# Feed-forward upward product: from one 32-bit product to three 16-bit products over a split activation

## The reference

```python
x = x + _L0_xattn_ref(_layernorm(x), ctx, ctx, Wq, Wk, Wv, Wo)
x = x + _L0_ffn_ref(_layernorm(x), W1, b1, W2, b2)
x = x + _L1_xattn_ref(_layernorm(x), ctx, ctx, mask, ...)
x = x + _L1_ffn_ref(_layernorm(x), ...)          # 8 experts, one per token

def _L0_ffn_ref(x, W1, b1, W2, b2):
    def _quantize(W):
        gamma = jnp.mean(jnp.abs(W))
        return jnp.clip(jnp.round(W / (gamma + EPS)), -1.0, 1.0)
    Wq1, Wq2 = _quantize(W1), _quantize(W2)
    h = relu(einsum('bsd,fd->bsf', x, Wq1) + b1)
    return einsum('bsf,df->bsd', h, Wq2) + b2
```

## Time and profile before

| what | us |
|---|---|
| median of 3 runs | 536.88 (535.7 to 539.16) |
| the profiled execution, its own time | 535.18 |
| its span, first to last instruction | 533.0 |
| PE busy in the span | 459.7 |
| POOL busy in the span | 359.5 |
| mean granted TensorE clock, as a share of full | 0.958 |

### The profile page before, as it was taken

How to read it: one execution, slowest core, us unless ns; L and a number is a source line. 1 busy time by engine, 2 the same in 40 slices (tenths; PEclk the granted TensorE clock), 3 DMA queues, 4 the chain that set the end, 5 groups by cost and what they waited for, 6 DMA issues and landing times.

```text
span 533.0 us, 19424 instructions
## 1 busy us (share of the span) xinstructions
PE 459.7 (86%) x6192; PEld 357.6 (67%) x6192; DVE 380.5 (71%) x1125; ACT 350.0 (66%) x872; POOL 359.5 (67%) x739
## 2 busy tenths in 40 slices
PE   3678999999988799998999999999978615999992
PEld 2456777777766699885566666666655405999991
DVE  6788888888986566535578888898898562555551
ACT  4366788888865556563677788788767713666661
POOL 5788887888842366577667776999986770555552
PEclk9799999999999999999799999999999955999997
DMA  7565445454432930034344444555442233444430
GB/s 182 146 160 147 109 121 124 115 138 114 124 77 59 337 85 0 1 91 104 94 114 119 127 122 113 149 146 146 126 126 70 74 121 86 106 108 108 106 99 23
DMA packets 103996, 60.18 MB, mean 113 GB/s; under 512 B 21234, under 2 KB 100098, under 8 KB 103922
## 3 DMA queue, kind: packets, MB, share of 16 engines
q1 hardware_dynamic: 100562, 51.92, 38.8%
q0 software_dynamic: 2784, 6.82, 3.7%
q10 hardware_dynamic: 576, 0.53, 0.3%
HBM read 20.03 MB, written 8.81 MB: 54 GB/s over the span
## 4 chain that ended last, share of the span: by engine, by line
PE 63%; POOL 11%; issue 8%; DVE 8%; DMA 5%; ACT 2%; SPq 1%; POOLq 0%; DVEq 0%; ACTq 0%
PE bank L702 8%; PE bank L923 6%; PE bank L845 5%; PE score L653 5%; PE scoreT L835 5%; PE scoreT L913 5%; PE bank L561 3%; POOL expert_rows L1341 3%; DVE negmax L1536 3%; PE bank L592 3%; PE bank L756 3%; DMA stack<-negpT 2%; PE scoreT L680 2%; PE score L913 2%; PE score L619 2%
## 5 line engine op out<-in xcount | busy, mean ns | idle before, releaser
L1536 DVE TENSOR_REDUCE negmax<-score 128x8 f32<-128x1024 f32 x128 | 156.2, 1220 | 36.1 <-PE score L653 34.1
L1028 ACT ACTIVATE P<-scoreT 128x1024 f32<-128x1024 f32 x128 | 131.7, 1029 | 51.4 <-PE scoreT L671 30.1
L702 PE MATMUL bank<-P,Vc 128*32 128x128 f32 x2048 | 69.2, 276 | 1.9 <-issue 1.8
L1420 POOL DMA_INDIRECT out<-by x39 | 37.5, 962 | 48.8 <-DVE by L1882 48.1
L702 PEld LDWEIGHTS bank<-P,Vc 128*32 128x32 f32 x2048 | 52.1, 109 | 15.4 <-issue 9.8
L653 PE MATMUL score<-stack 64*128 64x128 bf16 x1024 | 51.9, 222 | 6.9 <-DVE negmax L1536 4.5
L653 PEld LDWEIGHTS score<-stack 64*128 64x128 bf16 x1024 | 29.6, 95 | 37.8 <-issue 23.4
L1284 POOL TENSOR_TENSOR pieces<-rest,pieces 128x256 bf16<-128x256 f32 x63 | 42.8, 679 | 4.9
L1281 POOL TENSOR_TENSOR pieces<-full,pieces 128x256 bf16<-128x256 f32 x63 | 42.3, 672 | 4.7 <-ACT pieces L1008 4.4
L1282 POOL TENSOR_TENSOR rest<-full,pieces 128x256 f32<-128x256 f32 x63 | 42.5, 675 | 0.0
L923 PE MATMUL bank<-M,P 128*128 x312 | 41.5, 276 | 0.5 <-DVE by L1882 0.5
(11 more groups left out here) (215 smaller groups left out, 1220.0 us busy)
## 6 DMA issues: line engine op xcount, KB each, us to landing
stack<-pieces SPq DMA_DIRECT2D x192, 128.0 KB, 2.5
ctxT<-in_ctxT SPq DMA_DIRECT2D x32, 128.0 KB, 2.4
XB<-expert_rows SPq DMA_DIRECT2D x39, 66.0 KB, 2.1
XA<-expert_rows SPq DMA_DIRECT2D x39, 64.0 KB
XR<-in_x SPq DMA_DIRECT2D x4, 512.0 KB, 4.8
stack<-blank SPq DMA_DIRECT2D x32, 64.0 KB, 2.1
stack<-negpT SPq DMA_DIRECT2D x64, 32.0 KB, 1.9
ME<-in_M SPq DMA_DIRECT2D x1, 2048.0 KB, 9.9
```

The source lines that it names most:

```text
L702: mm = nc.tensor.matmul(PVOUT[VCOL * i:VCOL * (i + 1), half * 128:(half + 1) * 128], Vc[:, k % BODY, at:at + VCOL], P32[:, 2 * p_slot(L, k ...
L1028: nc.scalar.activation(P32[:, at:at + 2, :], SCORET[:], ACT.Exp, scale=SCALE).then_inc(sem("exp_done"), 1)
L1420: nc.gpsimd.indirect_dma_start(out=out, out_offset=bass.IndirectOffsetOnAxis(ap=at_, axis=0), in_=by[r][:, 0:D], in_offset=None).then_inc( ...
L1536: nc.vector.tensor_reduce(negmax[:, k % 2, :, half * HQ:(half + 1) * HQ], SCORE[:].rearrange("p r (h k) -> p r h k", h=HQ), AX.X, ALU.max, ...
```

## The change

`F1` quantized is written in 16 bits to `F1h`, which lies in the space of `W0`'s query weights. The activation `fxnT` (32-bit words) is taken as a sum of three 16-bit numbers: the upper half of each word, read in place with a step of two; the upper half of the rest (`frest` = fxnT minus that, on DVE, `take_high`); and what then remains (`flow`, on POOL, `take_middle`). `up` makes three products for each of the four chunks and adds them in PSUM. PE waits for `f_rest` and `f_low` as well as for `fxnT`. The buffers of `frest` and `flow` lie in `W0`, `cosT` and `sinT`, and in one new tile.

```diff
--- before.py
+++ after.py
@@ -175,6 +175,14 @@
         frstd = sb("frstd", [128, 2, 2])
         fxnT = sb("fxnT", [128, 2, PAIR])
         hT = sb("hT", [128, 2, FC, PAIR])
+        F1h = W0[:, 0:2, :].rearrange("p c n -> p (c n)").bitcast(BF16)
+        frest = [W0[:, 2:4, :].rearrange("p c n -> p (c n)"), sb("frest", [128, PAIR])]
+        flow = [cosT[:].bitcast(BF16), sinT[:].bitcast(BF16)]
+
+        def top_half(words):
+
+            return words.bitcast(BF16)[:, 1::2]
+
         qred = sb("qred", [128, 2])
         qgam = sb("qgam", [128, 2])
 
@@ -828,12 +836,16 @@
                 def up(p, b):
                     if is_pair(p):
                         pe.wait_ge(sem("f_xnT_ready"), p + 1)
+                        pe.wait_ge(sem("f_rest"), p + 1)
+                        pe.wait_ge(sem("f_low"), p + 1)
+                        parts = (top_half(fxnT[:, b, :]), top_half(frest[b][:]), flow[b])
                         for c in range(FC):
                             if c % 2 == 0:
 
                                 pe.wait_ge(sem("f_relu"), count(FC * (p - 1) + c + 2))
-                            mm = nc.tensor.matmul(f_hidden(p, c), F1[:, c * 128:(c + 1) * 128],
-                                                  fxnT[:, b, :], start=True, stop=True)
+                            for n, part in enumerate(parts):
+                                mm = nc.tensor.matmul(f_hidden(p, c), F1h[:, c * 128:(c + 1) * 128], part,
+                                                      start=(n == 0), stop=(n == len(parts) - 1))
                             if c % 2 == 1:
                                 mm.then_inc(sem("f_up"), 1)
 
@@ -1385,8 +1397,17 @@
                     x = X[:, 2 * p:2 * p + 2, :] if isinstance(p, int) else X[:, bass.ds(p * 2, 2), :]
                     nc.gpsimd.tensor_tensor(x, x, rowsb[:, 2:3, :].broadcast_to([128, 2, 128]), ALU.add).then_inc(sem("f_biased"), 1)
 
+            def take_middle(p, b):
+
+                if is_pair(p):
+                    pool.wait_ge(sem("f_rest"), p + 1)
+                    if p < 2:
+                        pool.wait_ge(sem("k_rotated"), 2 * PAIRS)
+                    nc.gpsimd.tensor_tensor(flow[b], frest[b][:], top_half(frest[b][:]), ALU.subtract).then_inc(sem("f_low"), 1)
+
             def ffn_step(p, b):
                 ffn_rstd(p + 4, b)
+                take_middle(p + 2, b)
                 ffn_bias(p + 2)
                 run_early(early, p)
                 if b == 1:
@@ -1402,7 +1423,8 @@
             body_loop(pool, step, START, {-2: partial(x_group, 2),
                                           B - 7: gate_norm,
                                           B - 3: partial(ffn_rstd, 0, 0), B - 2: partial(ffn_rstd, 1, 1),
-                                          B - 1: partial(ffn_rstd, 2, 0), B + 1: partial(ffn_rstd, 3, 1)})
+                                          B - 1: lambda: (ffn_rstd(2, 0), take_middle(0, 0)),
+                                          B + 1: lambda: (take_middle(1, 1), ffn_rstd(3, 1))})
             pool.wait_ge(sem("weights_loaded"), LOADED)
             pool.wait_ge(sem("ln_folded"), 3)
             ffn_bias(0)
@@ -1796,11 +1818,20 @@
                         run_early(early, p)
                     stats_of(p + 4, b)
                     normalise(p + 3, 1 - b)
+                    take_high(p + 2, b)
                     add(p)
                     x_stats(p)
                     if p == PAIRS - 1:
                         run_early(early, p)
 
+                def take_high(p, b):
+
+                    if is_pair(p):
+                        dve.wait_ge(sem("f_xnT_ready"), p + 1)
+                        if p == 0:
+                            dve.wait_ge(sem("k_projected"), PAIRS)
+                        nc.vector.tensor_tensor(frest[b][:], fxnT[:, b, :], top_half(fxnT[:, b, :]), ALU.subtract).then_inc(sem("f_rest"), 1)
+
                 def begin(p):
 
                     dve.wait_ge(sem("attn_added"), 2 * p + 2)
@@ -1813,7 +1844,7 @@
                     every_pair(step)
                     dve.wait_ge(sem("f_added"), 2 * PAIRS)
 
-                return begin, rest
+                return begin, take_high, rest
 
             def end_rows():
 
@@ -1947,7 +1978,9 @@
 
                 w = FW[i]
                 dve.wait_ge(sem(f"quant{i}"), 2)
-                nc.vector.tensor_scalar(w, w, BIG_ROUND, None, ALU.subtract).then_inc(sem("quantized"), 1)
+                if i == 0:
+                    dve.wait_ge(sem("q_projected"), PAIRS)
+                nc.vector.tensor_scalar((F1h, w)[i], w, BIG_ROUND, None, ALU.subtract).then_inc(sem("quantized"), 1)
 
             def quantize(i):
 
@@ -2013,10 +2046,10 @@
                 nc.vector.tensor_scalar(sums[:], rank[:], float(REGION // 128), None, ALU.mult).then_inc(sem("regions_set"), 1)
 
             early = attention(1)
-            begin, every = ffn(early)
+            begin, take_high, every = ffn(early)
             body_loop(dve, step, START, {-3: partial(x_group, 2), BODY - 1: sum_weights, B - 8: gate_square, B - 4: partial(begin, 0),
-                                         B - 3: partial(begin, 1), B - 2: partial(begin, 2), B: partial(begin, 3),
-                                         B + 1: regions_set})
+                                         B - 3: partial(begin, 1), B - 2: partial(begin, 2), B - 1: partial(take_high, 0, 0),
+                                         B: lambda: (take_high(1, 1), begin(3)), B + 1: regions_set})
             every()
             dve.wait_ge(sem("regions_set"), 2)
             body_steps(early, EARLY - AHEAD, LAST, {B + 5: end_rows})
```

## The result

The changed kernel took a median of 546.23 us in four executions (542.91 to 548.78). The kernel before took 537.63 us in four on the same chip (535.7 to 539.16). The ratio is 1.0136 with a 95% interval of 1.0093 to 1.0179, so the change costs **7.3 us, between 5.0 and 9.6** (the plain difference of these two medians is 8.6). The forecast was 542.1, or +5.2, with a range up to 547.0. Sign and place were right. The number is not that of the main case (540.8 to 542.3, 62% of the chances), but that of rival (c), the clock that falls where PE waits (545.5, 12%), and part 4 of the sum went the other way.

The account below looks back on a forecast made before the run. The feed-forward loop was taken as bound by PE's unbroken chain, 3.73 us per pair. Terms of 2.54 + 3.56 - 0.77 made 5.3; 5.2 was taken, giving 536.88 + 5.2 = 542.1 us, range 537.3 to 547.0.

Parts of the forecast that it names:

- main case: Whole kernel: the summed delays hold without any rival, 540.8 to 542.3 us; chance 62%.
- rival (c): The clock falls where PE now waits, costing up to 3.4 us, 545.5 us in all; chance 12%.
- part 4: Steps 10 to 15: a delay at pair 12, then savings in `up`; together -0.97 us, or -0.77 with meetings.
- sum of 5.3: Whole kernel: forecast slowdown in us with DVE and POOL holding each other up, 2.54 + 3.56 - 0.77.
- rival (b): In `up`, reading every second half-word is no faster than words: 0.86 us over forecast, 551.6 us in all; chance 8%.
- Prices: Unit costs: 0.108 us per 16-bit matmul, `up` 0.43 us less per pair, POOL subtraction 0.68, hand-over 0.05.
- the circle: Feed-forward loop: addition, statistics, POOL's instructions and subtraction, `up`, `down`, addition; double step forecast to grow from 7.46 to 8.15 us.
- Part 1: First product: PE waits for DVE's and POOL's subtractions and is through 2.04 us later.
- Part 2: Third product: PE waits for POOL again, bringing the shift to 2.12 us, or 2.54 if DVE first waits for POOL's power.
- Part 3: Loop, pairs 1 to 9: four longer double steps, +2.76 us without DVE and POOL meeting, +3.56 with it.
- Rival (a): Loop: POOL's operand comes in time, PE keeps its saving; 4.9 us faster, 532.0, or 530.0 with start hidden; chance 7%.
- Rival (d): The existing clock fall at 252 to 260 us does not come; 3.4 us less, 538.7 us in all; chance 11%.

Follow-up runs that it names:

- e8: The changed kernel with the second subtraction on DVE instead of POOL from pair 12 on; 545.51 us, 1.0124 of the kernel before.
- e5: The changed kernel with DVE's subtraction for pair 0 issued ahead of the quantization of F2; 544.46 us, 1.0099 of the kernel before.
- e7: The changed kernel with both subtractions on DVE and pair 0's first one ahead of the quantization of F2; 532.99 us, 0.9846 of the kernel before.
- e3: The changed kernel with all three products reading the upper halves, both subtractions and their waits left out; 532.73 us, 0.9863 of the kernel before.
- e2: The changed kernel with the second subtraction moved from POOL to DVE, so both on DVE; 539.10 us, 0.9974 of the kernel before.
- e11: The changed kernel run once more, unedited; 544.61 us, 1.0121 of the kernel before.

## Why the prediction was right, point by point

In the trace four errors turn the sum of 5.3 into 8.1: the start is 3.4 too low, part 4 1.3 too low, the first line of the table adds 1.0, and a missing clock fall at the end takes 2.9 off. That the result lies in the range is owed to the width that (c) gave it, and in part to errors that cancel. The sign given for rival (b), an `up` above 1.7 us, would have misled: `up` took 2.71 and 2.65 in two places, by the clock and not by the operand, since the same form takes 1.35 elsewhere in the same trace.

- **Prices.** A 16-bit matmul of 256 columns was put at 0.108 and is 0.112 to 0.113; `up` saves 0.38, not 0.43. POOL's subtraction is 0.61, not 0.68. The hand-over from POOL to PE is 0.23, not 0.05, the one estimate that missed by much. Together they explain why the circle is 8.33: PE starts 5.00 after the addition instead of 4.87, and takes 3.33 instead of 3.28.
- **Part 1** (first product +2.04): the wait is right (2.59 for 2.47). The step left out that the product itself would be at half clock: 1.2 to 1.35 us more, and 0.34 in what follows it. That the clock makes this, and not the wait alone, is shown by e8, with the same wait, the whole clock and 1.50 us; in e5 and e7, where PE waits for 0.40 us or not at all, it takes 1.50 and 1.34.
- **Part 2** (shift 2.12 or 2.54): PE waits for POOL there, as forecast, and again the clock falls behind the wait. This is rival (c), at two of the places where PE now waits. It was priced at up to 3.4 us, from another fall; the start is 5.90 - 2.54 = 3.4 over the forecast. That the two agree is luck: the price was one fall of 8 us, and here there are two shorter ones.
- **Part 3** (+3.56): 3.56 to the hundredth, but partly by luck. I had put 0.2 us per double step on DVE and POOL meeting. In the slot that I named, DVE's subtraction took 0.42 and POOL's power 1.02, as without each other, so that part is zero; the hand-over and the shorter saving took its place.
- **Part 4** (-0.97 or -0.77) **failed**: D9 to D15 is +0.52. The sentence "Later POOL has the time" was wrong. I had followed the delay of `cut` to the pieces and SP's copies, and not to ACT, which shares the order: its wait for POOL holds up the copy of `xnT`. The wait of PE there is 1.47, against this row of the kernel before:

```profile
235.90 0.61 PE L575 MATMUL bank<-Wc,xnT 128*128 128x8 f32 x4 [0.46 <-ACT xnT L987]
```

  That is 1.0 of the 1.29 missed. POOL's part of it is 0.66 to 0.76 us: in e3, without any subtraction, this wait is 0.81, and in e2, e7 and e8 it is 0.71 or 0.72. The rest comes from a PE that arrives earlier. Two smaller terms make up the remainder within 0.1, the wait in front of `up(12)`, 1.10 where 0.95 was forecast, and four savings of 0.38 instead of 0.43. e8 takes 1.5 us out of D9 to D13 in its trace.
- **Rival (a)** does not hold for the change, but is real if the split is hidden: e3 and e7 are 6.0 and 5.8 us below before by the medians (7.4 and 8.3 by the ratios), where it said 4.9 to 6.9.
- **Rival (b)** is refuted: 275 and 270 ns, a pitch of 0.112 for strided and dense. The rule of the Trainium skill (SBUF — State Buffer, section "SBUF: two separate sides", under "Door 1: The DMA port swizzle"), that steps within a 16-byte line are free, agrees with that.
- **Rival (d)** happened in the profiled execution, and e11, where the clock does fall there, shows that it is not tied to the change.

On meetings, the timeline of the changed kernel has both outcomes:

```profile
204.11 1.02 POOL L1251 TENSOR_TENSOR xrs<-xsd,powers 128x4 f32<-128x4 f32 x1
...
204.91 0.42 DVE L1833 TENSOR_TENSOR W<-fxnT 128x256 f32<-128x256 f32 x1
...
208.32 1.01 POOL L1244 TENSOR_TENSOR frstd<-frstd,powers 128x2 f32<-128x2 f32 x1
...
208.35 0.41 DVE L1833 TENSOR_TENSOR frest<-fxnT 128x256 f32<-128x256 f32 x1
```

The first pair overlaps and neither grows. In the second, DVE keeps its 0.41 and POOL's power takes 1.01 instead of the 0.70 at 206.13; a subtraction of 256 columns on both sides gives 0.88 for DVE's, at 245.73 above. The exclusive lock that the Trainium skill describes (SBUF — State Buffer, section "SBUF: two separate sides"), in which the later one blocks for the whole of the other, would have kept the instruction at 204.91 waiting until 205.13 and stretched it; the measurement shows no such wait, so where the page and this trace differ the trace decides: these two instructions, with 4 elements a partition on POOL's side, ran beside each other.

## What to carry to other kernels

Before an operand gets a helper instruction on another engine, find the slot in that engine's order and ask whether the slot's predecessor depends on the result of the product itself: here that closed a circle of 8.33 us around a PE that needs 6.72. The same instruction one place earlier saved 3.8 us in the loop, on an engine with room it cost the loop nothing, and a first operand made ahead of time saved 2.9 us at the start. When an engine's delay is followed, follow it into every engine that waits for it, and then to what stands behind that wait in its order.

## What was not expected of the hardware

- Twelve 16-bit matmuls of 256 columns took 1.35 us and eight records of the 32-bit product 1.73: 0.112 against 0.216, with weights loaded in between in both, so three 16-bit terms are cheaper than one 32-bit product by 22%.
- A first product that starts 3.05 us behind the last pass, with PE idle for 2.43 us, was followed by 1.2 GHz in both profiled executions of the changed kernel, and not in that of e8, which does the same up to pair 12. In the two executions of the changed kernel the low clock lasted about 3.4 and 6.8 us, read from windows of half a us. The granted clock after a wait is not a constant of the program.
- The hand-over from POOL to PE was 0.23 us in the chain; POOL to POOL and DVE to POOL 0.07.
